# Two edits to a neighbour attention on one NeuronCore: normalisation one pipeline step later, and the point's own term multiplied from its features

## The chip, the cores and the metric

The kernel runs as one program on one core of a Trainium2 chip. The metric is the device time of one execution in microseconds. The engines are TensorE (PE, with its weight loads shown apart as PEld), VectorE (DVE), ScalarE (ACT), GpSimd (POOL) and SyncE (SP), which issues most of the DMAs. They run asynchronously and are ordered by semaphores alone.

## The reference

The whole program is a small network of two layers: a point-cloud block, a self-attention, a low-rank MLP, a cross-attention, a state-space block and another MLP. The change touches the point-cloud block only. For eight batches of 512 points with C = 32 features each, and for four space-filling orders ("methods") of the points, every point takes a window of ten neighbours in that order. Its feature vector for each of the ten is the point's own features beside the neighbour's minus its own, for all four methods, 256 numbers in all, rounded to float16. An attention in heads of 32 runs among the ten rows of one point:

```
gf = concatenate([broadcast(center, (B, N, k, C)), neigh - center], axis=-1)
x16 = stack(per_method)[..., perm].reshape(B * N, k, 256).astype(float16)
qh = x16.reshape(B * N, k, nheads, 32)
scores = einsum('bihd,bjhd->bhij', qh, qh) / sqrt(32)
out = einsum('bhij,bjhd->bihd', softmax(scores), qh).reshape(B * N, k, 256)
fused = out @ W_lin.T + b_lin
h = einsum('oc,bnkc->bonk', W_conv, fused)
feats = lrelu(instance_norm(h, (2, 3))).max(axis=-1)
```

This is done twice: stage 0 from the input to O = 32 channels, stage 1 from those to O = 64 channels.

## The kernel before

**Layout.** The four methods' sorted features lie in `ext` (128 partitions: method x channel; the sorted order with padding) and the points' own features in `F4` (the same partitions, four copies of the 32 channels). A value that reaches the output is a sum of three parts: the attention's weighted sum of neighbours, the point's own term (its features rounded to float16 times one weight matrix, less its features times another), and a bias. Since softmax rows sum to one, the own term does not depend on the attention; it is the same for the point's ten window rows.

**Phase "weights"** (`phase_window_weights`, once a stage) multiplies features by combined weights ahead of the attention. PE makes small combined weights `wp` from `lin` and `convT`; DVE copies and masks them (`wd`, L742). Then, for two halves q of the batches and chunks of 128 sorted positions, PE makes the value rows `vp` (L716), ACT copies them to a ring of three `stage` buffers (L796), and SP writes them to DRAM (`scratch_values`, L811). In between, PE makes the own term `cp` with two fp32 matmuls a batch (L727, L728), DVE adds the bias (L761), POOL splits the sum into three bf16 pieces (L780 to L784), and SP writes those to `scratch_own` (L817). DVE also makes the low part of the features, `W["lo"]` (L767, L768).

**Phase "attend"** (`phase_window_attention`) runs over 44 blocks g: two halves of 22, each block 24 points (the last 8) of four batches. It is a software pipeline written out by hand: `ticks` calls, for every tick t and on every engine in a fixed order, the bodies with their lags, body(t - lag). POOL: `windows_minus_centre(t)` (L925; at the first block of a half ten small instructions more, L936 and L937) and `normalise(t - 2)` (L946). PE: `turn(t - 3)` (transposes, L994), `scores(t - 1)` (L974 adds the mask, L982 the products), `weigh(t - 3)` (the own term, L1010, then probabilities times values, L1021 or L1026). DVE: `sums(t - 2)` (L1097), `top_of(t - 1)` (L1079), `inverse(t - 2)` (L1104), `shift(t - 1)` (L1086), `take(t - 4)` in every second tick (statistics L1115 and maximum L1116, once per 128 outputs, so twice in stage 1). ACT: `bring(t - 3)` (L1046), `exponent(t - 1)` (L1039) and, for even g from 2 to 16, a masked copy for the second half (L1055, L1059). SP loads, for four blocks at a time and into a ring of two, the values in 16 DMAs (L906) and the own pieces in 3 (L911). Most buffers between engines are double; `prob` is triple.

The own term enters `weigh` as one bf16 matmul for every 128 outputs: the three pieces of 24 points (72 rows) are the stationary operand, a constant 0/1 matrix `ownhot` of 240 columns, ten for each point, moves through.

## Time and profile before

| | us |
|---|---|
| median of three runs | 1376.63 (1371.64 to 1384.47) |
| the profiled execution | 1368.01 |
| its span, first to last instruction | 1366.3 |
| granted TensorE clock, mean over the span | 0.857 |
| PE busy | 1014.2 |
| DVE busy | 768.7 |
| POOL busy | 443.7 |
| ACT busy | 442.1 |

The granted clock is a share of 2.4 GHz; over a short stretch it reads 1.00 or 0.50 (1.2 GHz), and something between where a stretch holds both. Busy time is that of the whole program; the phases here lie between 201 and 730 us of it. The times of rows are microseconds from the start of the span. PE's records of fp32 matmuls come as two instructions for each matmul of the program. Instructions on one engine overlap a little in the records, so the step from one start to the next is at times shorter than the duration beside it.

### The profile page before, as it was taken

How to read it: one execution, taken by the hardware profiler on the slowest of the kernel's cores; microseconds unless marked ns; L12 is line 12 of the kernel's file. 1: busy time of each engine (PE TensorE's matmuls, PEld its weight loads, DVE VectorE, ACT ScalarE, POOL GpSimd, SP SyncE). 2: the span in 40 equal slices, each digit the busy share in tenths (PEclk: the TensorE clock that was granted, in tenths of full speed). 3: DMA queues.
4: the chain of work that ended last, by engine and by line, in shares of the span. 5: the costliest groups of instructions: out<-in, count | busy, mean ns of one | idle time of the engine just before them, and what ended most of it. 6: DMA issues, size and time to landing. Idle time of an engine off the chain costs nothing. (4 is left out here: it accounts for less than half of the span.)

```text
span 1366.3 us, 28657 instructions
## 1 busy us (share of the span) xinstructions
PE 1014.2 (74%) x10354; PEld 751.7 (55%) x10354; DVE 768.7 (56%) x1848; ACT 442.1 (32%) x893; POOL 443.7 (32%) x366
## 2 busy tenths in 40 slices
PE   3772479366664893777673899994997799998698
PEld 2551249244543482555451799994743567775475
DVE  4869873476776844776775323236342356564542
ACT  0499511254333122452220122224001255663100
POOL 3000235777773467676750200000000054430000
PEclk9995596698897996885875899997997799998799
DMA  3851301222223033322310454540553435451000
GB/s 112 295 203 56 80 1 66 55 37 35 42 38 69 15 124 102 78 56 69 73 44 8 128 152 143 156 140 23 172 147 101 169 111 183 177 192 21 10 0 16
DMA packets 183727, 126.40 MB, mean 93 GB/s; under 512 B 99637, under 2 KB 157813, under 8 KB 182606
## 3 DMA queue, kind: packets, MB, share of 16 engines
q1 hardware_dynamic: 183082, 120.82, 30.1%
q10 hardware_dynamic: 548, 4.25, 0.8%
q8 instruction: 65, 1.06, 0.3%
q14 instruction: 32, 0.26, 0.1%
HBM read 110.27 MB, written 14.76 MB: 92 GB/s over the span
## 5 line engine op out<-in xcount | busy, mean ns | idle before, releaser
L925 POOL TENSOR_TENSOR attend_diff<-win_ext,win_F 128x960 f16<-128x960 f32 x88 | 163.2, 1855 | 0.0
L994 PE MATMUL attend_prob_t<-core_ident,attend_pnorm 124*128 124x124 f32 x344 | 65.4, 320 | 93.4 <-POOL attend_pnorm L946 93.3
L946 POOL TENSOR_TENSOR attend_pnorm<-attend_prob,attend_inv 124x480 f32<-124x480 f32 x88 | 86.7, 985 | 99.4 <-DVE attend_inv L1104 99.4
L1039 ACT ACTIVATE attend_prob<-attend_centred 124x480 f32<-124x480 f32 x88 | 52.2, 594 | 167.7 <-DVE attend_centred L1086 167.7
L1079 DVE TENSOR_REDUCE attend_top<-attend_score 124x32 f32<-124x480 f32 x88 | 56.6, 644 | 76.9 <-PE attend_score L982 76.7
L994 PEld LDWEIGHTS attend_prob_t<-core_ident,attend_pnorm 124*128 124x128 f32 x344 | 41.4, 159 | 105.9 <-POOL attend_pnorm L946 105.5
L360 ACT ACTIVATE sort_signs<-sort_keysB,sort_key 128x512 bf16 x128 | 90.5, 739 | 13.0 <-DMA sort_keysB<-scratch_keys 13.0
L610 PE MATMUL order_ordered<-order_place,order_own 128*32 128x512 bf16 x768 | 69.0, 401 | 23.3 <-POOL order_own L563 23.3
L1288 DVE TENSOR_SCALAR attn_qT<-proj_qp,attn_bq,attn_gq 128x256 f32 x32 | 17.4, 543 | 122.3 <-ACT attn_sq L1267 122.3
L593 DVE TENSOR_SCALAR order_place<-core_iota,points_rank 128x512 bf16<-128x512 f16 x256 | 73.6, 365 | 16.2 <-PE order_ordered L610 13.6
L1809 DVE TENSOR_REDUCE cross_negtop<-cross_score 128x1 f32<-128x512 f32 x64 | 44.2, 691 | 59.8 <-PE cross_score L1680 59.8
L1680 PE MATMUL cross_score<-cross_kT,cross_qblock 128*128 128x512 f32 x128 | 71.7, 644 | 5.7 <-ACT cross_prob L1745 3.0
L982 PEld LDWEIGHTS attend_score<-attend_hi,attend_diff 128*60 128x60 f16 x1376 | 55.6, 123 | 33.2 <-issue 33.2
L1097 DVE TENSOR_REDUCE attend_total<-attend_prob 124x32 f32<-124x480 f32 x88 | 56.0, 636 | 30.1 <-ACT attend_prob L1039 30.0
L1046 ACT COPY attend_probT<-attend_prob_t 128x496 f32<-128x496 f32 x88 | 49.2, 559 | 65.2 <-PE attend_prob_t L994 65.2
L1597 POOL TENSOR_TENSOR cross_raw<-cross_raw,binary_base 128x2688 f32<-128x2688 f32 x8 | 47.0, 5872 | 70.1 <-DMA cross_raw<-in_fw_dram 70.1
L610 PEld LDWEIGHTS order_ordered<-order_place,order_own 128*32 128x32 bf16 x768 | 41.0, 99 | 50.8 <-DVE order_place L593 27.4
L982 PE MATMUL attend_score<-attend_hi,attend_diff 128*60 128x60 f16 x1376 | 66.0, 210 | 0.0
L974 PE MATMUL attend_score<-core_mask,core_rowsof 128*128 128x480 bf16 x88 | 38.3, 435 | 35.5 <-POOL attend_diff L937 28.2
L1240 PE MATMUL proj_qp<-core_xnT,attn_wq 128*128 128x256 f32 x256 | 63.3, 391 | 1.4 <-DMA attn_wv<-in_Wv_dram 1.4
L982 PE MATMUL attend_score<-attend_lo,attend_diff 128*60 128x60 f16 x1376 | 64.2, 207 | 0.0
L1373 POOL COPY attn_attT<-att_flipped 32x512 f32<-32x512 f32 x4 | 2.4, 602 | 187.7 <-DVE att_flipped L1359 187.7
(323 smaller groups left out, 2467.6 us busy)
## 6 DMA issues: line engine op xcount, KB each, us to landing
binary_base<-in_fmean_dram SPq DMA_DIRECT2D x8, 1344.0 KB, 8.0
cross_raw<-in_fw_dram SPq DMA_DIRECT2D x8, 1344.0 KB, 11.0
attend_vT<-scratch_values SPq DMA_DIRECT2D x160, 60.0 KB
sort_ctxT<-in_ctxT_dram SPq DMA_DIRECT2D x8, 1024.0 KB, 6.1
attn_wq<-in_Wq_dram SPq DMA_DIRECT2D x32, 256.0 KB
attn_wk<-in_Wk_dram SPq DMA_DIRECT2D x32, 256.0 KB
attn_wv<-in_Wv_dram SPq DMA_DIRECT2D x32, 256.0 KB
att_wo<-in_Wo_dram SPq DMA_DIRECT2D x32, 256.0 KB, 2.6
```

What stands on the lines that cost most here:

```text
L360: nc.scalar.activation(signs[t][:], keysB[:, bass.ds(b * N + at * N, N)], ACT.Sign, scale=-1.0, bias=key[:].bitcast(F32)[:, bass.ds(b * KC ...
L593: vec.tensor_scalar(place[i % RING][:], W["iota"][:], T["rank"][:, bass.ds((b * KC) + (m * B * KC + t), 1)], None, ALU.is_equal).then_inc( ...
L610: mm = nc.tensor.matmul(ordered[u][m * C:(m + 1) * C, :], own[u][:, k, t, :], place[i % RING][:], start=(t == 0 and k == 0), stop=(t == KC ...
L925: ins = nc.gpsimd.tensor_tensor(diff[u][:, :, 0:size], spread, f.unsqueeze(3).to_broadcast([P, QB, size, WIN]), ALU.subtract)
L946: nc.gpsimd.tensor_tensor(pnorm[g % 2][:, 0:n, 0:K].rearrange("p r (h w) -> p r h w", w=SPAN), prob[g % 3][:, 0:n * HEADS].rearrange("p (r ...
L982: mm = nc.tensor.matmul(scoreP[u][b * STEP:b * STEP + SROWS, blk, r], diff[u][:, r, sub:sub + SUB].rearrange("p n i -> p (n i)"), part[q][ ...
L994: mm = nc.tensor.transpose(probP[u][:, x, :], pnorm[u][:, 2 * x:2 * x + 2].rearrange("p r w -> p (r w)"), T["ident"][0:MROWS, 0:MROWS])
L1039: nc.scalar.activation(prob[g % 3][:, 0:n], centred[g % 2][:, 0:n], ACT.Exp, scale=INV).then_inc(exp_done, 1)
L1079: vec.tensor_reduce(top[g % 2][:, 0:blocks_of(g) * HC], seen(g), AX.X, ALU.max).then_inc(top_done, 1)
L1097: vec.tensor_reduce(total[g % 2][:, 0:n], prob[g % 3][:, 0:n], AX.X, ALU.add).then_inc(sum_done, 1)
L1240: mm = nc.tensor.matmul(out[u][:], w[u][:, c, :], T["xnT"][:, c, :], start=(c == 0), stop=(c == KC - 1))
L1680: nc.tensor.matmul(scoreP[g % 2][:], qblock[u][:, g].rearrange("p r q -> p (r q)"), kT[u][:], start=True, stop=True).then_inc(score_made, 1)
```

## The change

Two edits are made together.

**Normalising a step later.** The lags become SCORE 1, SUM 2, NORM 3, TURN 4: POOL's normalise is called one tick later than DVE's inverse, and PE's turn and weigh, ACT's bring and DVE's take a tick later too. DVE's order in a tick becomes top_of, sums, shift, inverse, take. PE's mask matmul is issued ahead of the wait for the differences.

**Own term from the features.** The weights phase no longer makes, splits and stores an own term. It leaves two SBUF tensors instead: `FX`, which holds for each pair of batches the rounded features of both (on partitions 0 to 31 and 64 to 95) and the plain ones (32 to 63 and 96 to 127), and `WX`, block-diagonal combined weights. In `weigh` two fp32 matmuls (for each stage) multiply `WX` by 24 columns of `FX`, each read ten times in a row (a step of zero). The bias is left out of the sum, since the instance norm removes it from all but the mean; the last lines put the mean right. `scratch_own`, `ownhot`, their DMAs and the semaphores go.

```
-SCORE_LAG, SUM_LAG, TURN_LAG = 1, 2, 3
+SCORE_LAG, SUM_LAG, NORM_LAG, TURN_LAG = 1, 2, 3, 4
...
-        F16c = s.sb("F16c", [P, B, N], F16)
-        FR = s.sb("FR", [P, B, N])
+        F16c = s.sb("F16c", [P, KC, N], F16)
...
+                for strip in range(QB):
+                    for m in range(METHODS):
+                        nc.tensor.matmul(wp[strip * C:(strip + 1) * C, O:2 * O], columns(strip % 2, m), convT[:],
+                                         start=(m == 0), stop=(m == METHODS - 1))
...
-                        for r in range(QB):
-                            nc.tensor.matmul(cp[n % 2][:, r], FR[:, q * QB + r, at], wc[:], start=True, stop=False)
-                            mm = nc.tensor.matmul(cp[n % 2][:, r], F4[:, q * QB + r, at], wdn[:], start=False, stop=True)
-                        mm.then_inc(own_made, 1)
...
+                for s2 in range(2):
+                    centre = slice(s2 * 2 * C, s2 * 2 * C + C)
+                    go(vec.tensor_copy(F16s[centre, ..., 0:N], pairs[centre, s2, ..., 0:N]))
+                    vec.tensor_copy(FXs[centre, ..., 0:N], F16s[centre, ..., 0:N])
...
+                for s2 in range(2):
+                    less = slice(s2 * 2 * C + C, (s2 + 1) * 2 * C)
+                    go(nc.gpsimd.tensor_copy(FXs[less, ..., 0:N], pairs[less, s2, ..., 0:N]))
...
-                    for k in range(PIECES):
-                        sp.dma_start(own[u][k * SB:(k + 1) * SB, 0:sbs, :],
-                                     bass.AP(owns, at + k * QB * O, [[own_row, SB], [SB * own_row, sbs], [1, QB * O]])
-                                     ).then_inc(values_in[u], 16)
...
-                ticks((0, later_windows), (SUM_LAG, normalise))
+                ticks((0, later_windows), (NORM_LAG, normalise))
...
-                    for grp in range(G):
-                        nc.tensor.matmul(made[grp][:, c:c + n * BLK * WIN], own[part % VRING][:, k % VPART, grp * P:(grp + 1) * P],
-                                         own_hot[:, 0:n * BLK * WIN], start=True, stop=False, skip_group_check=True)
+                    for x in range(2):
+                        points = FX[:, q * 2 + x, k * SB:k * SB + n * BLK]
+                        dst, w = (made[0][x * 2 * O:(x + 1) * 2 * O], WX) if G == 1 else (made[x], WX)
+                        nc.tensor.matmul(dst[:, c:c + n * BLK * WIN], w[:], points.unsqueeze(2).to_broadcast([P, n * BLK, WIN]),
+                                         start=True, stop=False, skip_group_check=True)
...
-                ticks((SUM_LAG, sums), (SCORE_LAG, top_of), (SUM_LAG, inverse), (SCORE_LAG, shift), (TURN_LAG + 1, take))
+                ticks((SCORE_LAG, top_of), (SUM_LAG, sums), (SCORE_LAG, shift), (SUM_LAG, inverse), (TURN_LAG + 1, take))
...
+                go(vec.tensor_scalar(middle[:], mv[:, :, 0], bias[:], None, ALU.add))
+                go(vec.tensor_scalar(middle[:], middle[:], -1.0, bias[:], ALU.mult, ALU.add))
+                go(vec.tensor_tensor(moved[:], middle[:], rstd[:], ALU.mult))
```

## Rows read from the trace of the kernel before

**Rows 1.** Timeline of the weights phase, stage 0 (start, duration, engine, line, operands, count).
```profile
203.54 1.16 PE L716 MATMUL weights_vp<-weights_wd,win_ext 128*128 128x128 f32 x8 [1.50 <-DVE weights_wd L742]
...
209.37 2.06 PE L716 MATMUL weights_vp<-weights_wd,win_ext 128*128 128x128 f32 x8
...
242.30 0.43 SPq L811 DMA_DIRECT2D scratch_values<-weights_stage  x1
...
244.40 0.18 POOL L952 MEMSET attend_pnorm<- 124x32 f32 x2 [2.48 <-POOLq L695]
```

**Rows 2.** Table of windows: PE, PEld, DVE, ACT, POOL busy (instructions), clock, DMA share, GB/s.
```profile
204.00:247.00 43.00, 34.33 (x207) 32.89 (x205) 15.83 (x16) 8.41 (x12) 22.62 (x43) 0.67 0.19 71
```

**Rows 3.** Timeline of the weights phase, stage 1.
```profile
481.25 3.67 PE L716 MATMUL weights_vp<-weights_wd,win_ext 128*128 128x256 f32 x8 [1.73 <-DVE weights_wd L742]
...
490.01 1.95 PE L716 MATMUL weights_vp<-weights_wd,win_ext 128*128 128x256 f32 x8
...
521.14 0.18 POOL L952 MEMSET attend_pnorm<- 124x32 f32 x2 [2.81 <-POOLq L695]
```

**Rows 4.** Page, costliest groups: busy us, mean ns | idle before, releaser.
```profile
L925 POOL TENSOR_TENSOR attend_diff<-win_ext,win_F 128x960 f16<-128x960 f32 x88 | 163.2, 1855 | 0.0
...
L946 POOL TENSOR_TENSOR attend_pnorm<-attend_prob,attend_inv 124x480 f32<-124x480 f32 x88 | 86.7, 985 | 99.4 <-DVE attend_inv L1104 99.4
...
L1039 ACT ACTIVATE attend_prob<-attend_centred 124x480 f32<-124x480 f32 x88 | 52.2, 594 | 167.7 <-DVE attend_centred L1086 167.7
...
L1079 DVE TENSOR_REDUCE attend_top<-attend_score 124x32 f32<-124x480 f32 x88 | 56.6, 644 | 76.9 <-PE attend_score L982 76.7
```

**Rows 5.** Timeline of POOL: single starts of normalise (L946) in both stages.
```profile
327.61 1.00 POOL L946 TENSOR_TENSOR attend_pnorm<-attend_prob,attend_inv 124x480 f32<-124x480 f32 x1 [0.71 <-DVE attend_inv L1104]
...
351.37 1.00 POOL L946 TENSOR_TENSOR attend_pnorm<-attend_prob,attend_inv 124x480 f32<-124x480 f32 x1 [1.74 <-DVE attend_inv L1104]
...
415.31 1.00 POOL L946 TENSOR_TENSOR attend_pnorm<-attend_prob,attend_inv 124x480 f32<-124x480 f32 x1 [1.56 <-DVE attend_inv L1104]
...
551.14 1.00 POOL L946 TENSOR_TENSOR attend_pnorm<-attend_prob,attend_inv 124x480 f32<-124x480 f32 x1 [0.71 <-DVE attend_inv L1104]
...
612.30 1.00 POOL L946 TENSOR_TENSOR attend_pnorm<-attend_prob,attend_inv 124x480 f32<-124x480 f32 x1 [1.31 <-DVE attend_inv L1104]
...
635.38 1.00 POOL L946 TENSOR_TENSOR attend_pnorm<-attend_prob,attend_inv 124x480 f32<-124x480 f32 x1 [1.74 <-DVE attend_inv L1104]
...
710.12 1.00 POOL L946 TENSOR_TENSOR attend_pnorm<-attend_prob,attend_inv 124x480 f32<-124x480 f32 x1 [2.58 <-DVE attend_inv L1104]
```

**Rows 6.** Table of windows in the attention of stage 1, columns as rows 2.
```profile
640.00:660.00 20.00, 17.37 (x309) 12.11 (x301) 13.68 (x26) 5.32 (x10) 13.04 (x10) 0.53 0.24 57
660.00:680.00 20.00, 13.01 (x394) 9.31 (x394) 16.27 (x32) 6.43 (x11) 15.26 (x11) 1.00 0.27 63
```

**Rows 7.** Timeline of one tick of stage 1, granted clock 1.00, PE alone.
```profile
670.55 0.64 PE L994 MATMUL attend_prob_t<-core_ident,attend_pnorm 124*128 124x124 f32 x4 [1.16 <-POOL attend_pnorm L946]
...
671.94 0.38 PE L1010 MATMUL attend_outp<-attend_ownhot,attend_own 72*128 72x240 bf16 x2
...
672.25 0.69 PE L1026 MATMUL attend_outp<-attend_probT,attend_vT 64*64 64x60 f32 x32
```

**Rows 8.** Timeline of one tick of stage 1, granted clock 0.50, PE alone.
```profile
641.01 1.09 PE L994 MATMUL attend_prob_t<-core_ident,attend_pnorm 124*128 124x124 f32 x4 [0.52 <-POOL attend_pnorm L946]
...
643.42 0.58 PE L1010 MATMUL attend_outp<-attend_ownhot,attend_own 72*128 72x240 bf16 x2
...
643.93 1.13 PE L1026 MATMUL attend_outp<-attend_probT,attend_vT 64*64 64x60 f32 x32
```

**Rows 9.** DMA issues: line, count, KB each, median us to landing.
```profile
scratch_values<-weights_stage SPq DMA_DIRECT2D x8, 512.0 KB, 2.8
```

**Rows 10.** Groups by line and shape, ACT, 256 to 420 us, columns as rows 4.
```profile
L1055 ACT ACTIVATE attend_hi<-win_ext,core_headmask 128x2112 f16<-128x2112 f32 x4 | 8.2, 2040 | 0.0
```

**Rows 11.** Timeline of SP: the value loads of one part, stage 1.
```profile
665.31 9.40 SPq L906 DMA_DIRECT2D attend_vT<-scratch_values  x16
```

More of the change, by code:

```diff
@@ L698, in _, with columns @@
                 pe.wait_ge(L.loaded, 16 * 3)
-                for half in range(2):
-                    for m in range(METHODS):
-                        at = half * (METHODS * C) + perm.index(m)
-                        nc.tensor.matmul(wp[m * C:(m + 1) * C, half * O:(half + 1) * O],
-                                         lin[:, at:at + METHODS * (C - 1) + 1:METHODS], convT[:], start=True, stop=True)
-                pe.wait_ge(spread, 1)
-                nc.tensor.matmul(wp[:, 2 * O:3 * O], blb[:], convT[:], start=True, stop=True).then_inc(made, 1)
+                def columns(half, m):
+                    at = half * (METHODS * C) + perm.index(m)
+                    return lin[:, at:at + METHODS * (C - 1) + 1:METHODS]
+                for m in range(METHODS):
+                    nc.tensor.matmul(wp[m * C:(m + 1) * C, 0:O], columns(1, m), convT[:], start=True, stop=True)
+                for strip in range(QB):
+                    for m in range(METHODS):
+                        nc.tensor.matmul(wp[strip * C:(strip + 1) * C, O:2 * O], columns(strip % 2, m), convT[:],
+                                         start=(m == 0), stop=(m == METHODS - 1))
+                for at in range(0, P, O):
+                    mm = nc.tensor.matmul(wp[at:at + O, 2 * O:2 * O + 1], convT[:], bl[:], start=True, stop=True)
+                mm.then_inc(made, 1)
                 pe.wait_ge(split, 1)
@@ L801, in _ @@
             def _(sp):
-                sp.wait_ge(cleared, 1)
-                for q in range(HALVES):
-                    sp.dma_start(bass.AP(owns, (q * EXT + N) * own_row, [[own_row, tail], [1, own_row]]), empty[:]
-                                 ).then_inc(own_written[q], 16)
                 for q in range(HALVES):
@@ L855, in phase_window_attention @@
         vT = [s.sb(f"vT{u}", [P, VPART * PAIRBLK * SUBS, 2, P // 2 if G == 1 else O]) for u in range(VRING)]
-        own = [s.sb(f"own{u}", [PIECES * SB, VPART, QB * O], BF16) for u in range(VRING)]
-        own_hot = s.sb("ownhot", [PIECES * SB, SB * WIN], BF16)
         hi = [s.sb(f"hi{q}", [P, QB, HEADS, EXT], F16) for q in range(HALVES)]
@@ L865, in phase_window_attention @@
         room = s.sb("room", [P, NG])
+        middle = s.sb("middle", [P, NG])
+        moved = s.sb("moved", [P, NG])
+        FX, WX, bias = W["FX"], W["WX"], W["bias"]
         best = W["new"]
@@ L975, in scores @@
                                      T["mask" if k else "mask0"][:, 0:n * HC * SPAN], start=True, stop=False, skip_group_check=True)
+                    pe.wait_ge(diff_ready, g + 1)
                     for blk in range(n):
@@ L2249 @@
                "scratch_values": HALVES * EXT * HEADS * QB * 2 * C}
-    halves = {"scratch_own": HALVES * EXT * PIECES * QB * 2 * C}
     nc = _bacc.Bacc("TRN2", target_bir_lowering=False, num_devices=1)
@@ L2258 @@
         D[name] = nc.dram_tensor(name, [n], _mybir.dt.float32, kind="Internal").ap()
-    for name, n in halves.items():
-        D[name] = nc.dram_tensor(name, [n], _mybir.dt.bfloat16, kind="Internal").ap()
     D["out"] = nc.dram_tensor("out_0_dram", (8, 32, 512), _mybir.dt.float32, kind="ExternalOutput").ap()
```

112 lines of the change are left out of this document (26 added, 86 removed).

## Prediction

> **What bounds the kernel now.** I read the page first, then the waits, then a table of time windows for the two stages of the neighbour attention, and last the timelines of single stretches. PE is the busiest engine of the page, but that is an average over a dozen phases; the change touches four stretches only: "weights" and "attend", each for two stages (O = 32 and O = 64 output channels).
>
> Weights, stage 0, lasts from the first small matmuls just before 203.54 to 244.40, where POOL's first instruction of the attention starts [rows 1]. Between 204 and 247 PE is busy 34.3 us with a mean granted clock of 0.67 (1.0 is 2.4 GHz, 0.5 is 1.2 GHz), DVE 15.8 us, ACT 8.4 [rows 2]. So PE leads, and behind it SP's queue: its last issue starts at 242.30 and the attention 2.1 us later. Stage 1 lasts from 481.25 (PE's first value matmul) to 521.14 [rows 3].
>
> The attention runs 44 blocks g through a pipeline of ticks. The reader is to see one closed loop. POOL's normalise(g) (L946) lets PE turn g (L994); behind the turn, in PE's own order, stand the scores of g+2; DVE's maximum of those scores (L1079) stands in DVE's order ahead of inverse(g+1) (L1104); and that inverse is what POOL's next normalise waits for: 99.4 us in all [rows 4]. One round is one tick. In stage 0 it takes 3.55 us: 18 ticks between 351.37 and 415.31 take 63.9 us [rows 5]. In stage 1 DVE has twice the statistics and maxima to take every second tick: 15 ticks between 551.14 and 612.30 take 61.2 us (4.08 each), 18 between 635.38 and 710.12 take 74.7 (4.15) [rows 5]. No engine is full. POOL owes 1.86 + 0.99 = 2.85 us a tick [rows 4]. DVE in stage 1 is busy 16.3 of the 20 us from 660 to 680 [rows 6]; at 3.85 us a tick there (the mean of the two kinds) that is 5.2 ticks, so 3.1 us each. PE in stage 1 at the upper clock needs 2.39 us from the start of a turn (670.55) to the end of the weighing (672.25 + 0.69) [rows 7]; at the lower clock 4.05 (641.01 to 643.93 + 1.13) [rows 8].
>
> **The change, part by part.**
>
> *Weights phase.* The matmuls of L727 and L728 go, and with them DVE's sums, POOL's three-way splitting and ten SP issues a stage. What is left for PE are the value matmuls (L716): ten chunks of eight instructions. A chunk of stage 0 took 1.16 us at 203.54 and 2.06 us at the lower clock (209.37) [rows 1]. Ahead of them come fifteen more small matmuls, thirty instructions of a quarter of the columns: between nothing and 30 x 1.16 / 8 = 4.4 us; I take 1, and DVE's list before `split`, three instructions shorter, pays it back. Ten chunks take 12 us (all upper) to 20 us (all lower). The engine entered the phase at the upper clock and had lost it by 209.37, after waiting for DVE and running the first own-term matmuls, both of which go or shrink. I take 13 us: from 203.5 to 216.5. Then ACT's last copy, the SP issue and the 2.1 us of landing and phase change [rows 1]: about 220, against 244.4. **Gain 24** (18 to 26). The next to be late would be DVE: all that it does now is 15.8 us [rows 2], part of it goes and six small instructions come, so it ends by 218 and hides behind the writes. The two copies that POOL gets are of 2048 elements a partition; between one and two times L925's price for 960 two-input elements [rows 4], so 4 to 8 us, beginning at 202: hidden.
>
> *Stage 1.* A chunk is 3.67 us at the lower clock and 1.95 at the upper [rows 3]. One of the first and nine of the second: 21.2 us, to 502.5; then ACT, issue and landing, where a 512 KB write needs 2.8 us to land [rows 9]. ACT's ring of three lets a write start every 1.95 us without waiting for it. Start of the attention at about 505 against 521.1. **Gain 16** (12 to 18).
>
> *Attention, normalising a step later.* L946 of g now stands a tick further back, and DVE's inverse stands behind shift. The loop above now has two ticks for its work (norm 1.0, turn and scores 1.4, DVE's four 2.3, two of them of 0.64 [rows 4]: 4.7 us, so 2.4 a tick) and binds nobody. What is late next is the fullest engine. Stage 0: POOL, 2.85, say 2.9. But while ACT makes the second half's masked copies (L1055, L1059), 2.04 us in every second tick [rows 10], another two-tick loop goes turn and scores, DVE's three up to shift, the exponent (0.6 [rows 4]), the masked copy, ACT's copy (about the same 0.6), the weighing: 1.4 + 1.8 + 0.6 + 2.0 + 0.6 + 0.7 = 7.1, so 3.5 a tick. The first half of the blocks thus wins nothing. Second half: 18 x (3.55 - 2.9) = 12. The five ticks from 327.61 to 351.37 hold POOL's ten edge instructions and a stretch at the lower clock: 23.8 us against 17.8 at the usual pace [rows 5]; I give them 3. One more tick to fill and drain costs 2, three more tiny DVE instructions at the end 0.6. **Stage 0: 12** (0 to 16).
>
> *Own term.* It was one bf16 matmul of 240 columns per 128 outputs; it is two fp32 ones of 240 columns. Each fp32 matmul is two instructions in these records. The trace has no fp32 matmul on repeated columns. The nearest row is L716 with 256 columns: eight instructions in 1.95 us, or 3.67 at the lower clock [rows 3], so about 0.22 and 0.43 each, less a sixteenth. Four of them: 0.83 and 1.6 us in stage 1, against 0.31 and 0.51 from L1010 to L1026 now [rows 7, 8]. With 0.1 for the change of shape PE's tick grows to 2.39 + 0.6 = 3.0 us, or 4.05 + 1.2 = 5.2 at the lower clock. If the repeated read costs double, another 0.8; if it is cheaper (each value is fetched once), down to 0.4. I take the row. In stage 0 the two write different halves of the output partitions; side by side 0.4, one after the other 0.8: PE stays under POOL either way. What is queued behind them on PE, the weighing, has copied(g) to wait for anyway.
>
> The Trainium skill (TensorEngine Tiling, Key Properties) says that changing the tiling mode drains the engine; in stage 0 scores, own term and weighing would now all be 64 columns wide and two drains would go. The trace agrees as far as the 0.31 us from L1010 to L1026 are more than two matmuls of 240 columns need at 2.4 GHz, 0.2. By that rule PE's tick of stage 0 is 0.2 shorter, which changes only the slower rival below, by 9 us.
>
> *Stage 1.* DVE 3.1, PE 3.0, POOL 2.9: I take 3.15 at the upper clock, 3.55 while the masked copies run, 5.2 at the lower. In before the granted clock is 0.53 from 640 to 660 and 1.00 from 660 to 680 [rows 6]. With PE almost never idle I expect it back soon: two of the 18 later ticks and one of the 15 earlier ones low. 18 x 3.15 + 2 x 2.05 = 60.8 against 74.7: 14. 15 x 3.55 + 1.65 = 54.9 against 61.2: 6. The ticks between: nothing. Filling (own terms at the lower clock) costs 2, the extra tick 2, the tail 0.6. **Stage 1: 15.5** (-10 to 25).
>
> *Loads.* 16 issues for four ticks, three fewer than now. They take up to 9.40 us [rows 11]; with 2.8 to land [rows 9], 12.2, against 4 x 3.15 = 12.6: just hidden.
>
> Sum: 24 + 16 + 12 + 15.5 = 67.5 us. It is made against the profiled execution (1368.0, span 1366.3); the median of the runs, 1376.6, is 8.6 above that. 1376.6 - 67.5 = **1309**.
>
> **Rivals.**
> - *The clock stays up* (0.20). With no idle gaps both stages keep the upper level but for the fill: 4 + 2 more in stage 1, 5 in its middle, 2 in stage 0's, 2 in the weights: 1294. The Trainium skill (TensorE: Matmul & The Clock Gate, Part 1) describes exactly this, that idleness throttles and sustained work releases; against it here speaks that PE was busy 17.4 of the 20 us from 640 to 660 and had the lower clock for nearly all of them [rows 6].
> - *Another wait takes the loop's place* (0.20): the value loads. If issue and landing of 16 loads reach 14 us when they are packed closer, the tick stays at 3.55 and the attention pays only the fill: 40 less 2 leaves 1338. For it: the margin above is 0.4 us. Against it: three issues a part are gone.
> - *Repeated columns read slowly* (0.10): PE's stage 1 tick is 3.8; 18 ticks win 6 instead of 14, 15 lose 4: 1321.
> - *Slower than before* (0.03): PE held at the lower clock throughout. Stage 1 is then 44 x 5.2 = 229 us against 44 x 4.1 = 180 (+49), stage 0, with half the own term, 44 x 4.6 = 202 against 44 x 3.6 = 158 (+44); less 40: 1430. It decides only when nearly all ticks of both stages are low, as stage 1's +49 alone is eaten by 40 + 12.
> - *The change does less than it says* (0.02): the weights phase is held by its writes; 1330.
>
> **Numbers.** The forecast has 0.45. Its own range is 1298 to 1322. Range 1283 to 1342: it takes in the first three rivals. A measurement of this kernel tells about 1% (14 us) from no change: faster 0.94 (all cases but the slower one, less 0.03 for a mixture of the two rivals near 1338 with it), same 0.03, slower 0.03.
>
> **What would show it.** Right: the attention of stage 0 starts some 19 us after wd is made; POOL's normalise of stage 0 every 2.9 us in the second half and every 3.5 in the first; stage 1 near 3.1 with DVE or PE without gaps; L1010's successor at 0.2 us an instruction. Wrong: ticks still of 3.55 and a DMA named before the weighing (loads); own-term instructions of 0.4 us at clock 1.0 (repeated read); clock 0.5 over most of 530 to 700 (slower rival); or a weights phase in which ACT waits for writes.

## The result, and the profile after

| | before | after |
|---|---|---|
| median, runs side by side | 1376.3 (4 runs) | 1276.1 (4 runs) |
| ratio, 95% interval | | 0.9327 (0.9283 to 0.937) |
| the same comparison on another chip | 1368.5 | 1278.4; 0.9353 (0.9303 to 0.9404) |
| profiled execution, span | 1366.3 | 1281.9 |

The change makes the kernel 6.5 to 6.7% faster by the ratios, about 90 us; the medians of the first comparison are 100 us apart. The forecast was 1309 us with a range from 1283 to 1342. The median lies 33 us under the forecast and 7 under the range; by the ratio (0.9327 x 1376.6 = 1284) it lies at the range's lower edge. Three of the four phases gave more than was forecast, and one cost, late value loads, was priced at nothing. The two errors pull in opposite directions: without the part of that cost which the experiments below take away, the ratio is 0.9232 and the time 1271 us, outside the range. So it is in part luck that the result lies at the range's edge.

The changed kernel's page: busy time of each engine, then groups (busy us, mean ns | idle before, releaser). L881 is normalise, L860 the differences, L945 the new own term.

```profile
PE 987.0 (77%) x10374; PEld 726.2 (57%) x10374; DVE 760.1 (59%) x1840; ACT 436.9 (34%) x893; POOL 403.0 (31%) x292
...
L860 POOL TENSOR_TENSOR attend_diff<-win_ext,win_F 128x960 f16<-128x960 f32 x88 | 164.1, 1867 | 24.9 <-PE attend_score L917 24.5
...
L881 POOL TENSOR_TENSOR attend_pnorm<-attend_prob,attend_inv 124x480 f32<-124x480 f32 x88 | 87.0, 989 | 33.8 <-DVE attend_inv L1039 33.4
...
L945 PE MATMUL attend_outp<-stage_FX,stage_WX 128*64 128x240 f32 (+3 forms) x352 | 77.8, 405 | 11.4 <-DMA attend_vT<-scratch_values 11.1
```

Normalise waited 99.4 us for the inverse before [rows 4], now 33.4. A new wait has come on PE: L945 stands behind the value loads for 11.1 us.

Where the time went, in four phases. A weights phase runs from POOL's last instruction of the phase before it to its first of the attention, an attention phase from there to DVE's last normalising instruction.

| phase, us | before | after | difference | forecast |
|---|---|---|---|---|
| weights, stage 0 | 43.9 | 16.8 | -27.1 | -24 |
| attention, stage 0 | 183.4 | 165.3 | -18.1 | -12 |
| weights, stage 1 | 43.4 | 27.6 | -15.8 | -16 |
| attention, stage 1 | 207.4 | 185.3 | -22.1 | -15.5 |
| sum | | | -83.1 | -67.5 |

The spans differ by 84.4 us. The rest of the program, which the change does not touch, gives 1.3. In all the profiles of this case that rest takes between 879 and 895 us, so phases tell more than whole spans do.

Timeline of the changed kernel's weights phase, stage 0, against [rows 1]. It starts at 205.30:

```profile
207.56 0.73 DVE L716 TENSOR_SCALAR weights_wd<-weights_wp,core_headmask 128x32 f32<-128x32 f32 x4 [3.93 <-PE weights_wp L694]
...
208.34 9.65 PE L706 MATMUL weights_vp<-weights_wd,win_ext 128*128 128x128 f32 x80 [0.85 <-DVE weights_wd L716]
...
210.15 8.82 SPq L762 DMA_DIRECT2D scratch_values<-weights_stage  x10
...
217.29 4.56 DVE L730 TENSOR_TENSOR stage_lo<-win_ext,weights_high 128x4224 f16<-128x4224 f32 x1
...
222.12 0.18 POOL L887 MEMSET attend_pnorm<- 124x32 f32 x2 [12.04 <-POOLq L679]
```

The ten value chunks (L706) take 9.65 us, all at the upper clock. The engine that ends the phase is not SP but DVE: L730 makes the low part until 221.85, and the attention starts 0.3 later.

The same phase of stage 1, against [rows 3]. Here PE's 20.45 us and the writes behind them do end it:

```profile
440.41 20.45 PE L706 MATMUL weights_vp<-weights_wd,win_ext 128*128 128x256 f32 x80 [0.96 <-DVE weights_wd L716]
...
445.32 16.97 SPq L762 DMA_DIRECT2D scratch_values<-weights_stage  x10
...
464.27 0.18 POOL L887 MEMSET attend_pnorm<- 124x32 f32 x2 [22.73 <-POOLq L679]
```

Single starts of normalise (L881), against [rows 5]: blocks 18, 23 and 41 of stage 0, then of stage 1.

```profile
301.65 1.01 POOL L881 TENSOR_TENSOR attend_pnorm<-attend_prob,attend_inv 124x480 f32<-124x480 f32 x1 [1.05 <-DVE attend_inv L1039]
...
321.17 1.00 POOL L881 TENSOR_TENSOR attend_pnorm<-attend_prob,attend_inv 124x480 f32<-124x480 f32 x1 [0.18 <-DVE attend_inv L1039]
...
374.81 1.00 POOL L881 TENSOR_TENSOR attend_pnorm<-attend_prob,attend_inv 124x480 f32<-124x480 f32 x1 [1.95 <-DVE attend_inv L1039]
...
548.23 1.01 POOL L881 TENSOR_TENSOR attend_pnorm<-attend_prob,attend_inv 124x480 f32<-124x480 f32 x1 [0.86 <-DVE attend_inv L1039]
...
568.11 1.00 POOL L881 TENSOR_TENSOR attend_pnorm<-attend_prob,attend_inv 124x480 f32<-124x480 f32 x1 [1.31 <-DVE attend_inv L1039]
...
632.32 1.00 POOL L881 TENSOR_TENSOR attend_pnorm<-attend_prob,attend_inv 124x480 f32<-124x480 f32 x1 [3.14 <-DVE attend_inv L1039]
```

| us between starts of normalise | st. 0 before | after | st. 1 before | after |
|---|---|---|---|---|
| phase start to block 3 | 29.9 | 26.2 | 30.0 | 32.0 |
| block 3 to 18 (masked copies run) | 53.3 | 53.3 | 61.2 | 52.0 |
| 18 to 23 | 23.8 | 19.5 | 23.1 | 19.9 |
| 23 to 41 | 63.9 | 53.6 | 74.7 | 64.2 |
| 41 to the end | 12.5 | 12.6 | 18.4 | 17.3 |

One tick of stage 1 on PE, against [rows 7]:

```profile
595.79 0.64 PE L929 MATMUL attend_prob_t<-core_ident,attend_pnorm 124*128 124x124 f32 x4
...
597.18 1.08 PE L945 MATMUL attend_outp<-stage_FX,stage_WX 128*128 128x240 f32 x4
...
598.19 0.69 PE L961 MATMUL attend_outp<-attend_probT,attend_vT 64*64 64x60 f32 x32
```

From the turn's start to the end of the weighing 3.09 us (2.39 before); from L945 to L961 1.01 us for four instructions. The table of windows, against [rows 6] (PE, PEld, DVE, ACT, POOL busy, clock, DMA share, GB/s):

```profile
560.00:580.00 20.00, 13.10 (x237) 9.52 (x235) 13.05 (x24) 3.09 (x6) 10.33 (x8) 0.66 1.32 90
...
580.00:600.00 20.00, 19.61 (x469) 14.60 (x460) 18.83 (x38) 6.80 (x13) 17.33 (x13) 1.00 0.76 58
```

From 580 to 600 the clock is 1.00 and PE is busy 19.6 of 20 us, DVE 18.8. In the 20 us before, PE stands idle for 7 and the DMA share is 1.32 at 90 GB/s. (The share is the sum of the packets' times over the span of 16 engines; where it passes 1, packets overlap in the records.) In [rows 6] it was 0.24 to 0.27 at 57 to 63. Nothing in the prediction explains that rise.

### The profile page after: what moved, and what is told of

The parts are those of the page before. It is cut to its first block and busy times, and to the rows that moved or that the text cites. A ratio compares the mean times of both kernels' runs of the same rounds, so it can differ in the third digit from the quotient of the medians.

```text
span 1281.9 us, 28395 instructions
## 1 busy us (share of the span) xinstructions
PE 987.0 (77%) x10374; PEld 726.2 (57%) x10374; DVE 760.1 (59%) x1840; ACT 436.9 (34%) x893; POOL 403.0 (31%) x292
## 5 line engine op out<-in xcount | busy, mean ns | idle before, releaser
L860 POOL TENSOR_TENSOR attend_diff<-win_ext,win_F 128x960 f16<-128x960 f32 x88 | 164.1, 1867 | 24.9 <-PE attend_score L917 24.5
L881 POOL TENSOR_TENSOR attend_pnorm<-attend_prob,attend_inv 124x480 f32<-124x480 f32 x88 | 87.0, 989 | 33.8 <-DVE attend_inv L1039 33.4
L1226 DVE TENSOR_SCALAR attn_qT<-proj_qp,attn_bq,attn_gq 128x256 f32 x32 | 17.4, 543 | 121.7 <-ACT attn_sq L1205 121.7
L945 PE MATMUL attend_outp<-stage_FX,stage_WX 128*64 128x240 f32 (+3 forms) x352 | 77.8, 405 | 11.4 <-DMA attend_vT<-scratch_values 11.1
L917 PEld LDWEIGHTS attend_score<-attend_hi,attend_diff 128*60 128x60 f16 x1376 | 51.7, 116 | 41.4 <-issue 25.5
L917 PE MATMUL attend_score<-attend_hi,attend_diff 128*60 128x60 f16 x1376 | 61.9, 204 | 11.2 <-POOL attend_diff L860 8.0
L929 PE MATMUL attend_prob_t<-core_ident,attend_pnorm 124*128 124x124 f32 x344 | 60.3, 300 | 10.6 <-POOL attend_pnorm L881 10.3
L1184 PEld LDWEIGHTS proj_vp<-attn_wv,core_xnT 128*128 128x128 f32 x512 | 62.2, 192 | 1.7
L1637 PEld LDWEIGHTS cross_mix<-cross_val,cross_probT 128*128 128x128 f32 x512 | 63.0, 194 | 0.1
L1637 PE MATMUL cross_mix<-cross_val,cross_probT 128*128 128x16 f32 x512 | 62.6, 254 | 0.0
L1184 PE MATMUL proj_vp<-attn_wv,core_xnT 128*128 128x128 f32 x512 | 62.3, 275 | 0.0
L1178 PE MATMUL proj_kp<-core_xnT,attn_wk 128*128 128x256 f32 x256 | 61.4, 383 | 0.0
## 6 DMA issues: line engine op xcount, KB each, us to landing
cross_raw<-in_fw_dram SPq DMA_DIRECT2D x8, 1344.0 KB, 10.5
```

Source lines behind the costliest of these rows:

```text
L860: ins = nc.gpsimd.tensor_tensor(diff[u][:, :, 0:size], spread, f.unsqueeze(3).to_broadcast([P, QB, size, WIN]), ALU.subtract)
L881: nc.gpsimd.tensor_tensor(pnorm[g % 2][:, 0:n, 0:K].rearrange("p r (h w) -> p r h w", w=SPAN), prob[g % 3][:, 0:n * HEADS].rearrange("p (r ...
L917: mm = nc.tensor.matmul(scoreP[u][b * STEP:b * STEP + SROWS, blk, r], diff[u][:, r, sub:sub + SUB].rearrange("p n i -> p (n i)"), part[q][ ...
L929: mm = nc.tensor.transpose(probP[u][:, x, :], pnorm[u][:, 2 * x:2 * x + 2].rearrange("p r w -> p (r w)"), T["ident"][0:MROWS, 0:MROWS])
L945: nc.tensor.matmul(dst[:, c:c + n * BLK * WIN], w[:], points.unsqueeze(2).to_broadcast([P, n * BLK, WIN]), start=True, stop=False, skip_gr ...
L1178: mm = nc.tensor.matmul(out[u][:], w[u][:, c, :], T["xnT"][:, c, :], start=(c == 0), stop=(c == KC - 1))
```

## The experiments

The phases of each kernel, in us, measured as above; ratios are to the kernel before, on the same chip:

| kernel | weights 0 | attention 0 | weights 1 | attention 1 | ratio (95%) |
|---|---|---|---|---|---|
| before | 43.9 | 183.4 | 43.4 | 207.4 | 1 |
| changed | 16.8 | 165.3 | 27.6 | 185.3 | 0.9327 (0.9283-0.9370) |
| the changed kernel again | 16.8 | 162.8 | 26.5 | 183.1 | 0.9353 (0.9303-0.9404) |
| lag alone | 43.9 | 166.0 | 43.5 | 179.2 | 0.9653 (0.9587-0.9720) |
| own term alone | 17.1 | 181.7 | 26.5 | 200.1 | 0.9611 (0.9541-0.9682) |
| new lag, old DVE order | 16.9 | 160.1 | 27.3 | 184.7 | 0.9341 (0.9295-0.9386) |
| old lag, new DVE order | 16.8 | 243.9 | 27.5 | 238.1 | 1.0319 (1.0267-1.0371) |
| masked copies in halves | 16.8 | 156.0 | 26.5 | 180.2 | 0.9281 (0.9229-0.9334) |
| ring of three | 16.8 | 163.6 | 26.5 | 177.9 | 0.9274 (0.9220-0.9328) |
| before, shifted 32 bytes | 43.9 | 183.6 | 43.4 | 208.9 | 1.0027 (0.9992-1.0063) |
| bias 16 floats | 17.2 | 160.6 | 24.8 | 183.1 | 0.9342 (0.9295-0.9389) |
| bias 16 floats, halves | 16.8 | 152.9 | 27.3 | 181.8 | 0.9260 (0.9216-0.9303) |
| bias 48 floats | 16.8 | 162.0 | 24.8 | 172.3 | 0.9232 (0.9198-0.9266) |
| bias 48 floats, halves | 16.8 | 153.2 | 26.3 | 171.9 | 0.9187 (0.9147-0.9226) |

The changed kernel once more, beside its variants, for the spread between chips:

> The changed kernel once more, beside its variants on one chip. Both theories: the ratio measured first, 0.928 to 0.937; attention stage 1 about 186 us, value loads with a DMA share of 1.2 to 1.3 in the stretches in which two parts are loaded, PE's waits for values about 11 us in 3 or 4 waits.

**The lag alone** (in the kernel before).

```diff
-SCORE_LAG, SUM_LAG, TURN_LAG = 1, 2, 3
+SCORE_LAG, SUM_LAG, NORM_LAG, TURN_LAG = 1, 2, 3, 4
-                ticks((0, later_windows), (SUM_LAG, normalise))
+                ticks((0, later_windows), (NORM_LAG, normalise))
-                ticks((SUM_LAG, sums), (SCORE_LAG, top_of), (SUM_LAG, inverse), (SCORE_LAG, shift), ...
+                ticks((SCORE_LAG, top_of), (SUM_LAG, sums), (SCORE_LAG, shift), (SUM_LAG, inverse), ...
```

> The kernel before with the lags 1, 2, 3, 4, DVE's new order and the mask matmul ahead of the wait; own term and weights phases as before. Theory (the two edits act in different places and add up): attention stage 0 shorter by about 18 us, stage 1 by about 22, less what the three bf16 pieces' loads and the small own-term matmul change; weights phases unchanged at 43 to 44 us each; in all 36 to 46 us less than before (ratio 0.967 to 0.974). Rival A (the attention gained because the own term no longer comes out of DRAM): 0 to 15 us less, and the waits of normalise for the inverse fall without the tick getting shorter. Rival B (the later lag pays only as long as the loads are short, and with 19 issues a part instead of 16 the loads take the loop's place): 20 to 30 us less, with PE's wait for the values several times the 11 us of the changed kernel.

Waits of this kernel (total us, times, longest):

```profile
POOL attend_pnorm L946 <- DVE attend_inv L1104: 29.7, 44, 3.1
```

It gives 17.4 us in stage 0 and 28.2 in stage 1, 47 in all by the ratio. That is the theory, at a little more than its 36 to 46. Normalise's wait falls from 99.4 to 29.7 although the own term still comes from DRAM, so rival A is out. So is rival B: PE waits 7.1 us for a part's loads, less than in the changed kernel. Stage 1 is 6 us shorter than with both edits together, so something in the other edit takes back part of it.

**The own term alone** (changed kernel with lags 1, 2, 2, 3 and the old orders).

```diff
-SCORE_LAG, SUM_LAG, NORM_LAG, TURN_LAG = 1, 2, 3, 4
+SCORE_LAG, SUM_LAG, NORM_LAG, TURN_LAG = 1, 2, 2, 3
```

> The changed kernel with the lags put back to 1, 2, 2, 3, DVE's old order and the mask matmul behind the wait; the own term from the features stays. Theory (edits add up): weights stage 0 about 17 us and stage 1 about 27.5 as in the changed kernel, 43 us less for both; the attention as before within 4 us (the loop through normalise sets the tick, and two fp32 matmuls of 0.5 to 0.6 us each sit in front of the probabilities on PE only while the copied probabilities are awaited); in all 39 to 47 us less (ratio 0.966 to 0.972). Rival A (own term matters in the attention): 55 to 65 us less. Rival B (the fp32 matmuls lie in the loop as soon as PE is the one that normalise waits for): 25 to 35 us less, with stage 1's tick over 3.5 us.

```profile
POOL attend_pnorm L881 <- DVE attend_inv L1039: 89.2, 86, 5.1
```

Some 53 us, between the theory's 39 to 47 and rival A's 55 to 65: the weights phases as expected (43.7), and 9 more from the attention, 7.3 of them in stage 1. The loop through normalise is still there (89.2 us of waits). Its ticks of stage 1 alternate between 3.55 and 4.15 us where before many took 4.57; from 640 to 658 us of the kernel before, where four such ticks follow each other, the clock is 0.50. Over stage 1's attention the clock is 0.90 with the own term alone, 0.81 with the lag alone and 0.74 before:

```profile
475.00:675.00 200.00, 142.11 (x3144) 103.90 (x3144) 151.51 (x293) 71.81 (x101) 133.70 (x110) 0.90 0.57 55
```

```profile
504.00:683.00 179.00, 121.09 (x3056) 86.72 (x3056) 148.39 (x290) 69.55 (x101) 133.84 (x110) 0.81 0.30 71
```

```profile
521.00:729.00 208.00, 133.83 (x3056) 94.29 (x3056) 151.64 (x290) 72.30 (x101) 134.02 (x112) 0.74 0.26 61
```

The first fence is the own term alone, the second the lag alone, the third the kernel before. Each is one execution, and the clock varies between executions. Over the whole program it was 0.891 to 0.900 in all four of the own term alone, 0.859 to 0.867 in the four of the lag alone, and 0.830 to 0.861 in the eleven of the kernel before beside them. So the own-term edit goes together with more of the upper clock. Whether the fp32 matmuls in the tick are the cause was not tried.

**Which part of the lag edit.** The changed kernel with DVE's old order, and with the old lags and the new order.

```diff
-                ticks((SCORE_LAG, top_of), (SUM_LAG, sums), (SCORE_LAG, shift), (SUM_LAG, inverse), ...
+                ticks((SUM_LAG, sums), (SCORE_LAG, top_of), (SUM_LAG, inverse), (SCORE_LAG, shift), ...
```

> The changed kernel with DVE's old order sums, top_of, inverse, shift, take; the lags 1, 2, 3, 4 stay. Theory (the later lag is what breaks the loop through normalise, and what DVE does first in a tick matters little): within 4 us of the changed kernel in time, ticks of 2.8 to 3.0 us in stage 0's second half. Rival (with the old order sums waits for the exponent of the tick before and holds up top_of, so that the tick stays at DVE's and ACT's chain): ticks of 3.3 to 3.6, 15 to 25 us slower than the changed kernel.

```diff
-SCORE_LAG, SUM_LAG, NORM_LAG, TURN_LAG = 1, 2, 3, 4
+SCORE_LAG, SUM_LAG, NORM_LAG, TURN_LAG = 1, 2, 2, 3
```

> The changed kernel with the lags 1, 2, 2, 3; DVE's new order and the early mask matmul stay. Theory (the loop scores, top, inverse, normalise, turn closes in one tick, and now the inverse stands behind shift in it): ticks of 3.6 to 4.3 us in stage 0, attention of stage 0 180 to 200 us and of stage 1 200 to 220, 35 to 65 us slower than the changed kernel. Rival (DVE's order alone gives the gain): attention within 6 us of the changed kernel's 163 and 183 us.

The later lag gives the whole gain of this edit without DVE's new order (0.9341, against 0.9327 and 0.9353). Both kernels here keep the mask matmul ahead of the wait; what it is worth, no run separates. The new order with the old lags costs 98 us against the own term alone (1412.1 and 1314.2, on two chips; before was 1366 on both). That is some 135 us more than the changed kernel takes, where 35 to 65 were expected. The timeline shows why, DVE then POOL, in one tick of stage 1:

```profile
620.47 0.66 DVE L1014 TENSOR_REDUCE attend_top<-attend_score 124x32 f32<-124x480 f32 x1 [2.63 <-PE attend_score L917]
...
621.05 0.64 DVE L1032 TENSOR_REDUCE attend_total<-attend_prob 124x32 f32<-124x480 f32 x1
...
621.61 0.65 DVE L1021 TENSOR_TENSOR attend_centred<-attend_score,attend_top 124x480 f32<-124x480 f32 x1
...
622.17 0.34 DVE L1039 RECIPROCAL attend_inv<-attend_total 124x32 f32<-124x32 f32 x1
```

```profile
622.59 1.00 POOL L881 TENSOR_TENSOR attend_pnorm<-attend_prob,attend_inv 124x480 f32<-124x480 f32 x1 [1.83 <-DVE attend_inv L1039]
...
627.26 1.00 POOL L881 TENSOR_TENSOR attend_pnorm<-attend_prob,attend_inv 124x480 f32<-124x480 f32 x1 [1.83 <-DVE attend_inv L1039]
```

From the maximum (620.47) to normalise (622.59) are 2.12 us: maximum, sums, shift, inverse. In the kernel before the inverse stood right behind the maximum. The two instructions that now stand between (each 0.56 us from its start to the next) lie in the loop, so 3.55 + 1.12 = 4.67, and the step to the next normalise (627.26) is 4.67. In stage 1 nearly every tick now takes that, where 3.55 and 4.15 alternated. In stage 0 the ticks go from 3.55 to 4.67 and many to 5.7; in two of those, from 356.3 to 367.6 us, the clock is 0.50 and 0.55, and in the 4.67 us tick behind them 1.00. So part of stage 0's 62 us (243.9 against 181.7) goes with the lower clock. With the lag of 3 the same order costs nothing, since the loop has two ticks. The two orders then trade: the old one is 2.2 us shorter in stage 1's first 15 ticks (49.8 for 52.0), and alternates 4.0 and 2.8 us in the later ones, where the new one has 3.2 to 3.4 and 2.8.

**The masked copies in halves.** Each of ACT's eight copies is cut into two batches and two batches, and one runs in every tick from 2 to 17.

```diff
-                    if g % 2 or not 1 <= g // 2 <= 2 * HEADS:
+                    if not 2 <= g < 2 + 4 * HEADS:
                         return
-                    i = g // 2 - 1
+                    i, part = (g - 2) // 2, (g - 2) % 2
+                    rs = slice(part * (QB // 2), (part + 1) * (QB // 2))
```

> The changed kernel; each of ACT's eight masked copies of the second half (1.4 to 1.9 us, one in every second tick) is cut into two over two batches each, one in every tick from 2 to 17. Theory (in the first half of each stage a loop through ACT in the ticks with a copy sets the pace: ticks alternate 3.97 and 3.01 us in stage 0, 4.14 and 2.85 in stage 1, where later ticks take 2.80): the alternation goes, 15 ticks of stage 0 take 44 to 47 us for 53.4, of stage 1 46 to 49 for 52.0, in all 8 to 13 us less than the changed kernel. Rival (the first half is slower by ACT's total work and not by its place in the tick, or by the lower clock): no alternation but the same mean, 0 to 3 us less.

Starts of normalise in stage 0, first the changed kernel, then this one:

```profile
273.46 1.00 POOL L881 TENSOR_TENSOR attend_pnorm<-attend_prob,attend_inv 124x480 f32<-124x480 f32 x1 [0.20 <-DVE attend_inv L1039]
...
276.48 1.00 POOL L881 TENSOR_TENSOR attend_pnorm<-attend_prob,attend_inv 124x480 f32<-124x480 f32 x1 [0.19 <-DVE attend_inv L1039]
...
280.45 1.00 POOL L881 TENSOR_TENSOR attend_pnorm<-attend_prob,attend_inv 124x480 f32<-124x480 f32 x1 [0.19 <-DVE attend_inv L1039]
```

```profile
252.00 1.02 POOL L881 TENSOR_TENSOR attend_pnorm<-attend_prob,attend_inv 124x480 f32<-124x480 f32 x1
...
255.01 1.01 POOL L881 TENSOR_TENSOR attend_pnorm<-attend_prob,attend_inv 124x480 f32<-124x480 f32 x1 [0.15 <-DVE attend_inv L1040]
...
258.11 1.01 POOL L881 TENSOR_TENSOR attend_pnorm<-attend_prob,attend_inv 124x480 f32<-124x480 f32 x1 [0.20 <-DVE attend_inv L1040]
...
261.13 1.00 POOL L881 TENSOR_TENSOR attend_pnorm<-attend_prob,attend_inv 124x480 f32<-124x480 f32 x1 [0.18 <-DVE attend_inv L1040]
```

The steps 3.02 and 3.97 become 3.01, 3.10 and 3.02. Fifteen ticks take 45.0 us in stage 0 (51.2 to 53.3 before the edit) and 49.3 in stage 1 (52.0). The loop through ACT that the prediction named is thus shown by breaking it. Stage 1 gains less than half as much. By the ratios the kernel is 6 to 10 us faster than the changed one, where 8 to 13 were expected; the intervals of the ratios overlap. A second pair, side by side on one chip, agrees: the same cut in the kernel with 16 floats (below) takes the median from 1276.6 to 1266.4, and the attention from 160.6 to 152.9 us in stage 0 and from 183.1 to 181.8 in stage 1.

**A ring of three value buffers.**

```diff
-VRING = 2
+VRING = 3
```

> The changed kernel with a ring of three value buffers for two, so that each load of a part starts four ticks earlier. Theory (the 11.1 us that PE waits for values are loads that start too late: a part's 16 issues take 9 to 12 us and the parts about the middle of a stage have two to four ticks for them): the three waits go, 8 to 12 us less than the changed kernel, of which the tick gaps of 6.4 (stage 0 middle) and 9.6 us (stage 1 middle) give most, less 1 us for one more cleared buffer. Rival (the loads' slow landing is from their running side by side, and more of them side by side are slower still; or the chain behind has another bound that closes the gap): 0 to 4 us less.

PE's waits for the values, changed kernel and ring of three:

```profile
PE attend_outp L945 <- DMA attend_vT<-scratch_values: 11.1, 3, 5.4
```

```profile
PE attend_outp L945 <- DMA attend_vT<-scratch_values: 0.6, 1, 0.6
```

The waits go, and stage 1's attention is 5 to 7 us shorter; the ratio is 0.5 to 0.8% lower, of the order of its own uncertainty. So the loads are late. The run does not say why.

**Where the value ring lies.** The DMA share gave the clue: it is high in every kernel so far with the own term from features, and with the lag alone it is not. In the compiled program the value ring of stage 1 starts at byte 110,080 of a partition in the kernel before (a multiple of 512) and at 118,880 in the changed one. The new tiles stand ahead of it, and `bias`, one float wide, takes 32 bytes. The first idea, that a multiple of 64 matters, was tried from both sides:

```diff
-                    W["bias"] = v.sb("bias", [P, 1])
+                    W["bias"] = v.sb("bias", [P, 16])[:, 0:1]
```

> The changed kernel with the tile bias 16 floats wide instead of one, of which the first column is used. bias takes 32 bytes of each partition, so every tile behind it, the value ring vT among them, starts 32 bytes past a multiple of 64; with 16 floats vT starts at a multiple of 64 again, as in the kernel before. In kernels with the own term from the features the loads of the same values take about twice the DMA engines' time (0.59 of a stretch of 60 us with 13,920 packets, against 0.27 with 14,602 packets with the own term from DRAM). Theory (placement: a write of 128 or 256 bytes that starts off a multiple of 64 costs the DMA engines about twice the time): in the same stretch the share falls to 0.22 to 0.30, the median landing of a 60 KB load from 4.0 to 4.5 us to under 2.5, PE's waits for values from 11 to under 4 us, and the kernel is 6 to 10 us faster. Rival (16 issues a part instead of 19 lay the loads differently over the 16 engines): the share stays at 0.5 to 0.6 and the time is the same within 2 us.

and in the kernel before, whose only edit is one unused tile of 32 bytes:

```diff
                     W["lo"] = v.sb("lo", [P, B, EXT], F16)
+                    v.sb("shift", [P, 8])
```

> The kernel before with one unused tile of 8 floats ahead of the attention, so that the value ring starts 32 bytes past a multiple of 64; nothing else differs, the 19 loads a part and the own term from DRAM stay. Theory (placement): the DMA share of the stretches with value loads doubles, from 0.24 in 60 us to 0.45 to 0.6, and the time is 0 to 6 us longer, since before the parts had three to four ticks of 3.5 to 4.6 us to land. Rival (the count of issues a part): share and time as before within 2 us.

The second doubled the share and the first changed nothing. So the count of issues is not the cause, placement is, and 64 is not the measure. With one float the ring is 96 bytes past a multiple of 256. With 16 floats it is at 118,912, 128 bytes past a multiple of 256. With 48 it is at 119,040, a multiple of 256 and not of 512:

```diff
-                    W["bias"] = v.sb("bias", [P, 1])
+                    W["bias"] = v.sb("bias", [P, 48])[:, 0:1]
```

> The changed kernel with bias 48 floats wide. The value ring of stage 1 then starts at a multiple of 256 bytes (that of stage 0 at one of 512); with one float it started 32 past a multiple of 64 and with 16 floats 128 past a multiple of 256, and both had a DMA share of 0.50 to 0.54 in a stretch of stage 1 with 14,239 to 16,072 packets, where the kernel before (ring at a multiple of 512) had 0.24 with 13,241. Stage 0, with packets of 128 bytes, had 0.19 to 0.23 at every placement. Theory (a 256-byte packet that lies across a 256-byte boundary of SBUF costs about twice): share 0.24 to 0.30 in stage 1, landing of the 60 KB loads under 2.6 us for 4.1, PE's waits for values 10.8 to under 6 us, stage 1's attention 4 to 8 us shorter than 183. Rival A (the boundary is at 512): share still 0.5 to 0.6. Rival B (share and landing fall, but the waits come from the issue of 16 loads taking 7 to 9 us, not from the landing): waits and time as before within 2 us.

The DMA queue (packets, MB, share of 16 engines) and the loads (median us to landing, where it was found) in 60 us of stage 1: the kernel before, before shifted, changed, 16 floats, 48 floats.

```profile
q1 hardware_dynamic: 13241, 3.40, 24.1%
...
attend_vT<-scratch_values SPq DMA_DIRECT2D x41, 60.0 KB
```

```profile
q1 hardware_dynamic: 15072, 3.84, 53.8%
...
attend_vT<-scratch_values SPq DMA_DIRECT2D x48, 60.0 KB
```

```profile
q1 hardware_dynamic: 14239, 3.40, 50.1%
...
attend_vT<-scratch_values SPq DMA_DIRECT2D x52, 60.0 KB, 4.0
```

```profile
q1 hardware_dynamic: 16059, 3.84, 54.2%
...
attend_vT<-scratch_values SPq DMA_DIRECT2D x58, 60.0 KB, 3.8
```

```profile
q1 hardware_dynamic: 17111, 4.09, 29.9%
...
attend_vT<-scratch_values SPq DMA_DIRECT2D x61, 60.0 KB, 2.4
```

| ring of stage 1 starts at | share x 60 us x 16 / packets |
|---|---|
| multiple of 512 (before) | 17.5 ns |
| 32 past that (before, shifted) | 34.3 ns |
| 96 past a multiple of 256 (changed) | 33.8 ns |
| 128 past a multiple of 256 (16 floats) | 32.4 ns |
| multiple of 256 (48 floats) | 16.8 ns |

Most of these packets are 256-byte pieces of the value rows. A piece that lies across a multiple of 256 in SBUF costs about twice the engine time. Stage 0 has pieces of 128 bytes; worked out in the same way from 40 us of it, they cost 12.2 to 12.5 ns in the kernel before, the shifted one, the changed one and the one with 16 floats. The Trainium skill (DMA: Bandwidth & Descriptors, How a descriptor splits into AXI transactions) cuts a read at 256-byte boundaries, so that a piece of 256 bytes which starts off them takes two transactions. The doubling measured here, on the writing side, agrees with that. Its rule would also charge half of the 128-byte pieces for a second one where the ring starts 32 or 96 bytes off (the kernel before, shifted, and the changed one), and no such cost showed.

The price in time depends on the cover, that is on how long the ticks leave a load to land. In the kernel before, the shift cost nothing that the ratio can tell (1.0027, 0.9992 to 1.0063). It was not free: PE's waits for a part's loads, which end there with an own piece, grow, before and shifted:

```profile
PE attend_outp L1010 <- DMA attend_own<-scratch_own: 3.1, 2, 1.6
```

```profile
PE attend_outp L1010 <- DMA attend_own<-scratch_own: 7.7, 3, 5.5
```

The 5.5 us lie in the filling of stage 1. In the changed kernel the placement cost about 1% (0.9232 against 0.9327 and 0.9353) and 11 to 13 us of stage 1's attention, 3 to 4 of them in the filling. That is more than the waits alone (9 of the 11.1 us lie in stage 1, and 2.0 of them are left): while PE stands, the clock falls to 0.66 (560 to 580), where with the ring at a multiple of 256 it is 1.00 from 480 to 607, the same blocks included. Stage 1 is then 35.1 us shorter than before, nearly the sum of the two single edits, 28.2 + 7.3.

**Both improvements.**

> bias 48 floats wide and ACT's masked copies in halves. Theory (placement and copies are separate costs): 4 to 8 us less than with the copies in halves alone, 14 to 18 us less than the changed kernel. Rival (landing is not what PE waits for): as with the copies in halves alone, 8 to 12 us less than the changed kernel.

1257.3 us beside 1366.0: ratio 0.9187 (0.9147 to 0.9226), the fastest kernel of the case, 1.5 to 1.8% under the changed kernel. By the ratios it is 19 to 23 us under the changed kernel, where 14 to 18 were expected. With 16 floats and halves the same expectation had failed the other way: 12 us under the changed kernel instead of 14 to 20 (1266.4 us beside 1278.4). There 16 floats had not mended the placement, and the DMA share was 0.57 over 60 us of stage 1. Beside the placement alone (1262.1) the copies give 4.8 us, at the edge of what these runs can tell; the phases put 8.8 us into stage 0's attention and lose 1.5 in stage 1's weights phase, which the edit does not touch.

## Where the prediction held and where it was off, step by step

- *Weights, stage 0 (24; measured 27.1).* The mechanism held. The value matmuls were priced at 13 us with part of them at the lower clock; all ran at the upper one, 9.65. That is below the 12 us named for it: a chunk's 1.16 us [rows 1] is its length, and the step from one chunk to the next is 0.97. "DVE ends by 218 and hides behind the writes" failed: DVE ends at 221.85, 16.6 us into the phase, and is the last. The four casts that build `FX` (2.08, 1.22, 1.22, 1.22) stand ahead of the low part on DVE and were counted only as "six small instructions". From wd to the attention 14.6 us, said 19. POOL's two copies took 3.83 us, hidden.
- *Weights, stage 1 (16; 15.8).* PE's chunks took 20.45 us, said 21.2.
- *Attention, stage 0 (12; 18.1).* The ticks were right: 3.55 in the first half with the masked copies (said 3.5), 2.80 in the second (said 2.9) but for one gap of 6.4 behind the value loads. The middle gave 4.3 (said 3). The term that failed is filling: one tick more was priced at +2, but the ticks of the fill themselves shrink, 4.6, 5.3 and 3.5 to 2.8, 2.9 and 2.8, and what lies ahead of the first normalise grows by only 1.2 with the extra tick in it. So -3.7 stands where +2 stood; the drain stayed.
- *Attention, stage 1 (15.5; 22.1).* Three ticks were priced at the lower clock, 6 us; the clock was 1.00 from 500 to 560 and from 580 to 632. The early ticks took 3.47 (said 3.55 and one at 5.2), so 9.2 and not 6. The middle gave 3.2 and not nothing. The later ticks gave 10.5 of the 14 forecast: without one gap of 9.6 us they were 3.2 each (said 3.15). Filling and draining, priced at 4.6, cost 0.9; with the ring at a multiple of 256 the filling is 2.3 us shorter than before, so the shorter ticks help here too. "PE almost never idle, so the clock comes back" is what stage 1 shows, and it was priced too timidly as a rival of its own.
- *Own term (0.83 us for four instructions).* 1.01 from start to start with the change of shape, said 0.93; PE's tick 3.09, said 3.0. Inside the row at 597.18 the starts lie 0.31, 0.20 and 0.20 us apart. That is 0.203 for 240 repeated columns, against 0.216 for the 256 plain ones of L706 at clock 1.00, and 0.216 x 15/16 is 0.2025. So repeated columns cost nothing, and that rival is out. The first and the last step are 0.1 longer, where one 0.1 was priced. In stage 0 the two run side by side: about 0.55 us. There the score matmuls and the own term now have the same shape, and the step between them is 0.02 us where it is 0.12 in stage 1; the forecast had named that effect, and it changed nothing in the time, since POOL sets the tick.
- *Loads ("12.2 against 12.6, just hidden").* Wrong, and the one cost priced at nothing. The landing was taken from a write of 512 KB; the median of the loads was 4.0 to 4.5 us and not 2.8, and PE waited 11.1 us. With the ring at a multiple of 256 it is 2.4, and 4.4 us of waits are left. The cause lay in no row of before. It was in the diff, as a new tile ahead of the ring, and in the addresses of the compiled program.
- *Rivals.* "The clock stays up" (0.20, 1294) came nearest. The loads did take something, but the tick did not stay at 3.55. PE at the lower clock throughout did not come about.
- *Open.* Whether PE's work on the own term keeps the clock up, and how much room PE has in stage 1, was not measured. With 48 floats both PE and DVE are full in its later ticks:

```profile
560.00:580.00 20.00, 19.86 (x491) 14.87 (x480) 20.00 (x41) 7.52 (x14) 17.61 (x14) 1.00 0.30 68
```

PE is busy 19.86 and DVE 20.00 of 20 us, so the next edit to stage 1 probably has to take work from both.

## What to carry to other kernels

When a loop is closed by an in-order engine, count which instructions stand inside it: giving the loop one more tick was worth 47 us, while moving two instructions into it cost 98, part of it by the lower clock that came with the longer ticks. A pipeline that gets a stage longer but ticks faster can also fill faster. Tiles that a DMA writes in pieces of 256 bytes belong on multiples of 256: a one-float tile allocated ahead of them moves everything behind it, and most of the bill comes only when the ticks get short enough to need the loads.

## What the runs showed of the hardware

- DMA pieces of 256 bytes into SBUF: 17 ns of engine time each on a multiple of 256, 32 to 34 ns at 32, 96 or 128 bytes past one; pieces of 128 bytes took 12.2 to 12.5 ns and showed no such cost.
- An fp32 matmul whose moving columns are each read ten times in a row (step zero) costs what plain columns do: at clock 1.00 one of its two instructions takes 0.203 us from start to start at 240 columns, against 0.216 at 256 plain ones.
- Two fp32 matmuls a stage-1 tick in place of two bf16 ones did not lower the granted clock; over stage 1's attention it was 0.90 with them and, in two kernels without them at the same lags, 0.74 and 0.78 (before, and before shifted).
